# Cross-attention and FFN on one core: loops unrolled, tiles turned by transposing DMAs instead of TensorE, mask added by a matmul, projections woven into the softmax steps

## Chip, core and metric

The kernel runs on one core of a Trainium2 chip. The metric is the device time of one execution in microseconds (us). The kernel before takes 1211.33 us, the median of 3 runs (1210.6 to 1213.23).

## What is computed

For 16 sequences of 128 tokens with 1024 features (2048 rows in all) and a context of the same size:

```python
x = x + xattn(layernorm(x), ctx, ctx, w_q, w_k, w_v, w_out, mask)   # 32 heads of 32, 8 key/value groups of 4 heads
x = x + ffn(layernorm(x), w12, b12, w3, b3)
# xattn: softmax(where(mask, q k^T / sqrt(32), finfo.min)) v, then @ w_out.T
# ffn:   x1, x2 = split(x @ w12.T + b12); (silu(x1) * x2) @ w3.T + b3
```

Everything is float32. The kernel keeps that precision by splitting each operand of a matmul into a high and a low float16 part (hi = f16(v), lo = f16(v - hi)) and by summing three products, hi*hi + hi*lo + lo*hi. Weights and context are scaled by a power of two beforehand, which is found from their largest magnitude (the kernel calls that a "top").

## The kernel before, in words

**Attention** goes over 8 blocks of 256 tokens (two sequences). Block t is projected while block t-1 attends. One iteration of the loop has 12 steps; in step s TensorE computes the scores of head group s (`scores`, L855), turns the probabilities of group s-2 from [query, key] to [key, query] with 8 f32 transposes (`turn_prob`, L867), weighs the values of group s-3 (`weigh`, L883), turns the attention output of group s-4 (`turn_attn`, L894), and computes one unit of the projections of block t (`product`, L812, 24 matmuls: 8 chunks of the contraction by 3 products). After the 12 steps it turns the normalised rows of block t+1 (`turn_x`, 16 transposes, L910) and does the four units of the output projection of block t-1 in a row (`out_proj`, L812 on `arena_out`). Iterations 2 to 6 are one hardware loop (`Fori`), as on every engine.

VectorE adds the mask while it takes the row maximum, one instruction of 128x128 per head (`row_maxima`, L1145, 64 a block), ScalarE applies exp per head (`exps`, L661, 64 a block), and the high and low parts of the turned probabilities are made from PSUM (`prob_hi`, L670, ScalarE; `prob_lo`, L1157, VectorE). The q and k parts are stacked to 96 partitions (hi, lo, hi against hi, hi, lo) by 24 and 12 small DMAs per block (`stack_q`, L387; `stack_k`, L395), because the stacks put other partitions under each other. GpSimd splits the context with 3 instructions per quarter (`split_ctx`, L536 to L540) and takes the inverse square roots of the layernorm (L524).

**Weights.** wq, wk, wv and wo are split chunk by chunk between the projections of block 0 and in iteration 1 (`high` L614 on ScalarE, `chunk_lo` L1092 on VectorE); their largest magnitude goes through TensorE (`turn_top`, `spread_top`, L788, L792). For w12 one common scale is found by reading all of it once during iterations 2 to 6 (`look_at_w12`, L1251, a 128x4096 reduction each), and it is loaded again and split in iterations 7 and 8 and in the first FFN block.

**FFN** goes over 4 blocks of 512 rows: 16 units of `product` for the hidden layer (24 matmuls of 128x512 each), 16 transposes of the next block's rows (`turn_y`, L1009), one unit of the output, 16 more transposes, 7 more units of the output.

The order of the work on each engine is written out by hand. One DMA queue, SP's, issues all transfers in program order; a wait in it holds all that is behind. The PSUM banks are: two for scores, two for turned probabilities, one for `weigh`, one for turned attention, two for projections.

Of the kernel before, what the change touches and what calls it, by code (L numbers as in the profile page):

```python
# [17 lines left out]

# [11 lines left out]
RMAX = bass.bass_isa.ReduceOp.max  # L31
# [19 lines left out]
VW = DH + 2  # L51
# [12 lines left out]
NDMA_STACK = 12  # L64


def xattn_ffn(nc, x, ctx_t, mask, wq_t, wk_t, wv_t, wo_t, w12_t, b12_t, w3_t, b3_row, out):
    x_blocks = x.rearrange("(b u p) d -> b p u d", b=NB, p=P)
    x1_dram = nc.dram_tensor("x1_scratch", (TOK, D), F32, kind="Internal").ap()
    x1_blocks = x1_dram.rearrange("(b u p) d -> b p u d", b=NB, p=P)  # L70
    x1_ffn = x1_dram.rearrange("(b u p) d -> b p u d", b=NF, p=P)
    out_ffn = out.rearrange("(b u p) d -> b p u d", b=NF, p=P)

    def at(blocks, i):

        return blocks[bass.ds(i, 1)].rearrange("o p u d -> (o p) u d")

    with ExitStack() as stack:
# [5 lines left out]


        arena_in = sb("arena_in", [P, 32768], F16)
        arena_out = sb("arena_out", [P, 16384], F16)
        arena_work = sb("arena_work", [P, 32768], F16)
        wstage = sb("wstage", [P, 4096], F32)

        def carve(arena, at_, n, dt=F16):

            w = n * (2 if dt is F32 else 1)
            v = arena[:, at_:at_ + w]
            return (v.bitcast(dt) if dt is F32 else v), at_ + w

        o = 0
        wq, o = carve(arena_in, o, 2 * GROUPS * KC * P)
        wq = wq.rearrange("p (s m c o) -> p s m c o", s=2, m=GROUPS, c=KC)
        ctx_in, o = carve(arena_in, o, KC * AB, F32)  # L100
        wk, o = carve(arena_in, o, 2 * KC * KV)
        wk = wk.rearrange("p (s c o) -> p s c o", s=2, c=KC)
        wv, o = carve(arena_in, o, 2 * KC * KV)
        wv = wv.rearrange("p (s c o) -> p s c o", s=2, c=KC)
        ctx, o = carve(arena_in, o, 2 * KC * AB)
        ctx = ctx.rearrange("p (s c n) -> p s c n", s=2, c=KC)
        wo = arena_out[:, :].rearrange("p (h s c o) -> p h s c o", h=2, s=2, c=KC)
        w12 = arena_in[:, :].rearrange("p (m s c o) -> p m s c o", m=MC, s=2, c=KC)
        w3 = wo

        o = 0
        x_in, o = carve(arena_work, o, U * D, F32)
        x_in = x_in.rearrange("p (u d) -> p u d", u=U)
        x_res, o = carve(arena_work, o, U * D, F32)
        x_res = x_res.rearrange("p (u d) -> p u d", u=U)
        xn, o = carve(arena_work, o, 2 * KC * AB)
        xn = xn.rearrange("p (s c n) -> p s c n", s=2, c=KC)
        q_part, o = carve(arena_work, o, 2 * 2 * 4 * AB)  # L120
        q_part = q_part.rearrange("p (r s g n) -> p r s g n", r=2, s=2, g=4)
        assert o <= 2 * FT * D + 2 * KC * FB, o
        o = 2 * FT * D + 2 * KC * FB
        q_stack, o = carve(arena_work, o, HEADS * AB)
        q_stack = q_stack.rearrange("p (g j n) -> p g j n", g=GROUPS, j=HPG)
        k_stack, o = carve(arena_work, o, GROUPS * AB)
        k_stack = k_stack.rearrange("p (b g n) -> p b g n", b=2, g=GROUPS // 2)
        v_aug, o = carve(arena_work, o, 2 * U * GROUPS * VW)
        v_aug = v_aug.rearrange("p (s u g w) -> p s u g w", s=2, u=U, g=GROUPS)
        attn_t, o = carve(arena_work, o, 2 * GROUPS * AB)  # L130
        attn_t = attn_t.rearrange("p (s g n) -> p s g n", s=2, g=GROUPS)
        assert o <= arena_work.shape[1], o
        score = sb("score", [P, 4, U, HPG * SEQ], F32)
        prob_t = sb("prob_t", [P, 2, 2, U, HPG * SEQ], F16)
        attn = sb("attn", [P, 2, U * HPG * DH], F32)
        k_part = sb("k_part", [P, 2, 2, AB], F16)


        o = 0
        y_in, o = carve(arena_work, o, FT * D, F32)  # L140
        y_in = y_in.rearrange("p (u d) -> p u d", u=FT)
        yn, o = carve(arena_work, o, 2 * KC * FB)
        yn = yn.rearrange("p (s c n) -> p s c n", s=2, c=KC)
        hid, o = carve(arena_work, o, 2 * MC * FB)
        hid = hid.rearrange("p (s c n) -> p s c n", s=2, c=MC)
        y_res, o = carve(arena_work, o, FT * D, F32)
        y_res = y_res.rearrange("p (u d) -> p u d", u=FT)
        assert o <= arena_work.shape[1], o
        silu = prob_t[:, :, :, :, :].rearrange("p a b c d -> p (a b c d)")[:, 0:2 * 2 * FB].bitcast(F32) \
            .rearrange("p (r n) -> p r n", r=2)  # L150
        gated = score[:, 0, :, :]
        b3_all = score[:, 2, :, :].rearrange("p u n -> p (u n)")


        ident = sb("ident", [P, P], F32)
        mask_u8 = sb("mask_u8", [P, SEQ], U8)
        mask_add = sb("mask_add", [P, SEQ], F32)
        b12 = sb("b12", [P, 2 * MC], F32)
        b2_scaled = sb("b2_scaled", [P, MC], F32)
        NW = 5 + 2 + 4 + MC + 4  # L160
        NSCALE = NW - (MC - 1)
        CH_K, CH_V, CH_O = 3, 6, 7
        CH_12, CH_3 = CH_O + 4, CH_O + 4 + MC
        w_max = sb("w_max", [P, NSCALE], F32)
        w_top = sb("w_top", [P, NSCALE], F32)
        w_exp = sb("w_exp", [P, NSCALE], F32)
        w_inv = sb("w_inv", [P, NSCALE], F32)
        w_scale = sb("w_scale", [P, NSCALE], F32)
        ctx_max = sb("ctx_max", [P, 1], F32)
        ctx_top = sb("ctx_top", [P, 1], F32)  # L170
        ctx_exp = sb("ctx_exp", [P, 1], F32)
        ctx_inv = sb("ctx_inv", [P, 1], F32)
        ctx_scale = sb("ctx_scale", [P, 1], F32)
        score_base = sb("score_base", [P, GROUPS], F32)
        out_base = sb("out_base", [P, 4], F32)
        c_score = sb("c_score", [P, GROUPS], F32)
        c_neg = sb("c_neg", [P, GROUPS], F32)
        c_out = sb("c_out", [P, 4], F32)
        ctx_exp_kept = sb("ctx_exp_kept", [P, 1], F32)
        w12_part = sb("w12_part", [P, 1], F32)  # L180
        c_hid = sb("c_hid", [P, 1], F32)
        c_hid_inv = sb("c_hid_inv", [P, 1], F32)
        hid_scale = sb("hid_scale", [P, 1], F32)
        c_ffn = sb("c_ffn", [P, 4], F32)
        bound = sb("bound", [P, 8], F32)
        row_max = sb("row_max", [P, 4, U * HPG], F32)
        neg_max = sb("neg_max", [P, 4, U * HPG], F32)
        inv_sum = sb("inv_sum", [P, U * HPG], F32)
        stats = sb("stats", [P, 2, 6], F32)
        moments = sb("moments", [P, 2, 2], F32)  # L190
        var_scaled = sb("var_scaled", [P, 2], F32)
        rstd = sb("rstd", [P, 2], F32)
        minus_half = sb("minus_half", [P, 1], F32)
        ones = sb("ones", [1, P], F32)
        w_one = sb("w_one", [1, CH_12], F32)
        ctx_one = sb("ctx_one", [1, 1], F32)


        bank = [stack.enter_context(nc.psum_tensor(f"bank{i}", [P, HALF], F32)) for i in range(8)]
        B_SCORE, B_TURN, B_AV, B_ATTN_T, B_DENSE = bank[0:2], bank[2:4], bank[4], bank[5], bank[6:8]  # L200
        B_FFN = bank[4:8]
        B_XT = bank[0:4]


        s_mask, s_b12, s_b3 = sem("mask_loaded"), sem("b12_loaded"), sem("b3_loaded")
        s_wload = [sem(f"weights_loaded_{i}") for i in range(8)]
        s_wload += [sem(f"weights_loaded_{i}") if i in (11, 14, 15) else None for i in range(8, 16)]
        s_wlook, s_w12max, s_w12init = sem("w12_looked_at"), sem("w12_max_step"), sem("w12_max_init")
        s_wmax, s_wtop, s_wscale = sem("w_max_done"), sem("w_top_done"), sem("w_scale_done")
        s_wrow, s_wone, s_ctxrow, s_ctxone = sem("w_max_turned"), sem("w_one_done"), sem("ctx_turned"), sem("ctx_one_done")  # L210
        s_whi, s_wready = sem("w_hi_done"), sem("w_ready")
        s_wscaled, s_wpool = sem("w_scaled_on_pool"), sem("w_ready_on_pool")
        s_ident, s_vinit, s_ones = sem("ident_done"), sem("v_init_done"), sem("ones_done")
        s_xfirst = sem("first_row_tile_loaded")
        s_xload, s_ctxload, s_xres = sem("x_loaded"), sem("ctx_loaded"), sem("x_res_loaded")
        s_ctxmax, s_ctxtop, s_ctxscale = sem("ctx_max_done"), sem("ctx_top_done"), sem("ctx_scale_done")
        s_ctxhi, s_ctx = sem("ctx_hi_done"), sem("ctx_ready")
# [19 lines left out]

        block = stack.enter_context(nc.Block())

        def dense0(t):
# [1235 lines left out]
```

## Time and profile before

| | us |
|---|---|
| median of 3 runs | 1211.33 |
| the profiled execution, its own time | 1213.68 |
| its span, from the first to the last instruction | 1211.9 |
| TensorE busy in the span | 1136.6 (94%) |
| VectorE, ScalarE, GpSimd busy | 656.9, 457.2, 202.3 |
| mean granted TensorE clock, share of full speed | 0.965 |

A start-to-start time tells what a matmul costs in a stream of them; its own duration is longer, since matmuls overlap. The chain of waits merges them without overlap, so its pieces add up. Busy times of VectorE also count overlapping instructions once, so that single durations times their number can come to more than the busy time.

### The profile page before, as it was taken

The numbers are of one execution on the slowest core, as the hardware profiler recorded it, in microseconds if no ns is written. First come the engines' busy times: TensorE is split into PE (matmuls) and PEld (weight loads), VectorE is DVE, ScalarE is ACT, GpSimd is POOL, SyncE is SP. The second block draws the span as 40 slices with busy tenths as digits, with TensorE's granted clock in tenths as the row PEclk, the third lists the DMA queues.
The fourth block names the chain that finished last, engine by engine and source line by source line (L and its number), as shares of the span: only waits on it lengthen the run. The fifth ranks groups of instructions, "written<-read, shape, count | busy, mean of one in ns | idle before, by whom it ended". The sixth has DMA issues, their size and how long they took to land.

```text
span 1211.9 us, 22281 instructions
## 1 busy us (share of the span) xinstructions
PE 1136.6 (94%) x8377; PEld 719.4 (59%) x8377; DVE 656.9 (54%) x2130; ACT 457.2 (38%) x978; POOL 202.3 (17%) x167
## 2 busy tenths in 40 slices
PE   4768899999999999999986998899999999999998
PEld 3557759779596887958755443444445444544443
DVE  5468849688696877968798244631233123411111
ACT  3448719357291854818586112200111011101100
POOL 2304004031040402204143000400030003003000
PEclk9788899999999999999995998899999999999999
DMA  6442314323423333334360250004000300011001
GB/s 242 143 154 68 102 32 142 119 104 93 149 91 108 124 110 142 84 119 166 97 257 1 102 194 35 1 35 174 1 1 35 141 32 0 17 67 54 1 18 52
DMA packets 55113, 109.35 MB, mean 90 GB/s; under 512 B 6288, under 2 KB 37008, under 8 KB 50448
## 3 DMA queue, kind: packets, MB, share of 16 engines
q1 hardware_dynamic: 55056, 108.58, 25.8%
q8 instruction: 38, 0.62, 0.2%
q14 instruction: 19, 0.16, 0.0%
HBM read 76.05 MB, written 16.78 MB: 77 GB/s over the span
## 4 chain that ended last, share of the span: by engine, by line
PE 78%; DVE 11%; issue 5%; POOL 3%; ACT 3%; DMA 0%; DVEq 0%; ACTq 0%; POOLq 0%
PE bank L812 66%; PE bank L867 3%; DVE score L1145 2%; PE bank L883 2%; PE bank L910 2%; PE bank L855 1%; PE bank L894 1%; DVE stats L1098 1%; DVE prob_t L1157 1%; PE bank L1009 1%; ACT arena_in L614 1%; POOL arena_in L540 1%; DVE arena_out L1092 1%; POOL arena_in L536 1%; POOL arena_in L538 1%
## 5 line engine op out<-in xcount | busy, mean ns | idle before, releaser
L812 PE MATMUL bank<-arena_work,arena_in 128*128 128x256 f16 (+1 forms) x3072 | 529.4, 334 | 16.9 <-DVE arena_in L1092 8.7
L812 PEld LDWEIGHTS bank<-arena_work,arena_in 128*128 128x128 f16 x3072 | 306.1, 100 | 226.1 <-issue 20.4
L812 PE MATMUL bank<-arena_out,arena_work 128*128 128x512 f16 x1536 | 334.8, 379 | 0.1
L661 ACT ACTIVATE score<-score,neg_max,c_score 128x128 f32<-128x128 f32 x512 | 205.8, 497 | 148.7 <-DVE neg_max L1151 148.6
L812 PEld LDWEIGHTS bank<-arena_out,arena_work 128*128 128x128 f16 x1536 | 150.2, 98 | 178.0 <-issue 0.5
L1405 DVE SCALAR_TENSOR_TENSOR score<-bank,b_scaled,prob_t 128x512 f32<-128x512 f32 x32 | 24.0, 750 | 205.9 <-PE bank L812 197.3
L1145 DVE CUSTOM_DVE_ANT_0 score<-bank,mask_add 128x128 f32<-128x128 f32 x512 | 113.1, 287 | 18.0 <-PE bank L855 12.8
L524 POOL TENSOR_TENSOR rstd<-var_scaled,minus_half 128x1 f32<-128x1 f32 x32 | 29.4, 918 | 465.6 <-DVE var_scaled L1104 465.6
L759 ACT ACTIVATE prob_t<-bank,b,c_hid 128x512 f32<-128x512 f32 x32 | 24.8, 776 | 202.0 <-PE bank L812 202.0
L812 PE MATMUL bank<-arena_in 128*128 128x256 f16 x768 | 92.2, 278 | 2.6 <-issue 2.6
L1431 DVE SCALAR_TENSOR_TENSOR arena_work<-bank,c_ffn,arena_work 128x256 f32<-128x256 f32 x64 | 28.0, 479 | 118.3 <-PE bank L812 118.3
L1157 DVE TENSOR_TENSOR prob_t<-bank,prob_t 128x512 f16<-128x512 f32 x128 | 81.9, 680 | 9.3 <-ACT prob_t L670 9.1
L867 PE MATMUL bank<-ident,score 128*128 128x128 f32 x512 | 73.0, 286 | 12.5 <-DVE prob_t L1157 9.1
L812 PEld LDWEIGHTS bank<-arena_in 128*128 128x128 f16 x768 | 76.3, 100 | 12.8 <-issue 2.8
L762 ACT ACTIVATE arena_work<-score,hid_scale 128x512 f16<-128x512 f32 x32 | 23.1, 722 | 150.5 <-DVE score L1405 150.5
L536 POOL TENSOR_TENSOR arena_in<-arena_in,ctx_scale 128x512 f16<-128x512 f32 x32 | 34.3, 1070 | 258.7 <-DVE ctx_scale L1246 258.7
L670 ACT ACTIVATE prob_t<-bank 128x512 f16<-128x512 f32 x128 | 69.5, 596 | 10.7 <-PE bank L867 10.6
L867 PEld LDWEIGHTS bank<-ident,score 128*128 128x128 f32 x512 | 58.6, 146 | 16.1 <-ACT score L661 8.2
L1210 DVE SCALAR_TENSOR_TENSOR arena_work<-bank,c_out,arena_work 128x256 f32<-128x256 f32 x64 | 28.0, 479 | 72.4 <-PE bank L812 72.4
L883 PE MATMUL bank<-arena_work,prob_t 128*128 128x34 f16 x1536 | 49.5, 179 | 3.8 <-DVE arena_work L1210 2.4
L883 PEld LDWEIGHTS bank<-arena_work,prob_t 128*128 128x128 f16 x1536 | 48.9, 97 | 5.8 <-DVE arena_work L1210 2.6
L589 POOL TENSOR_TENSOR arena_work<-arena_work,score 128x1024 f32<-128x1024 f32 x16 | 39.4, 2495 | 62.7 <-DMA arena_work<-x_scratch 62.7
(104 smaller groups left out, 936.0 us busy)
## 6 DMA issues: line engine op xcount, KB each, us to landing
arena_work<-x SPq DMA_DIRECT2D x15, 1024.0 KB, 5.3
arena_work<-x_scratch SPq DMA_DIRECT2D x7, 2048.0 KB, 12.1
arena_work<-arena_work SPq DMA_DIRECT2D x192, 64.0 KB, 2.0
wstage<-w_t SPq DMA_DIRECT2D x5, 2048.0 KB, 7.6
wstage<-w_t SPq DMA_DIRECT2D x9, 1024.0 KB, 6.9
arena_in<-ctx_t SPq DMA_DIRECT2D x8, 1024.0 KB, 5.0
x_scratch<-arena_work SPq DMA_DIRECT2D x8, 1024.0 KB, 4.0
out<-arena_work SPq DMA_DIRECT2D x16, 512.0 KB, 2.6
```

The lines of the kernel that those rows point to most:

```text
L524: pool.tensor_tensor(rstd[:, r:r + 1], var_scaled[:, r:r + 1], minus_half[:, :], ALU.pow)\
L536: pool.tensor_tensor(hi, ctx_in[:, cols], spread, ALU.mult).then_inc(s_ctxhi, 1)
L589: ins = pool.tensor_tensor(y_res[:, u], y_res[:, u], b3_all, ALU.add)
L661: ins = act.activation(s, s, ACT.Exp, bias=neg_max[:, m % 4, HPG * u + j:HPG * u + j + 1], scale=c_score[:, m:m + 1])
L670: act.activation(prob_t[:, m % 2, 0, u], B_TURN[u][:, :], ACT.Copy).then_inc(s_pthi, 1)
L812: ins = pe.matmul(dst, lhs(a, c), rhs(b, c), start=(c == 0 and n == 0), stop=(c == KC - 1 and n == 2))
L867: ins = pe.transpose(B_TURN[u][:, SEQ * j:SEQ * j + SEQ], score[:, m % 4, u, SEQ * j:SEQ * j + SEQ], ident[:, :])
L883: ins = pe.matmul(dst, prob_t[:, m % 2, p, u, SEQ * j:SEQ * j + SEQ], v_aug[:, v, u, m], start=(n == 0), stop=(n == 2))
L1145: ins = dve.tensor_tensor_reduce(score[:, m % 4, u, SEQ * j:SEQ * j + SEQ], B_SCORE[u][:, SEQ * j:SEQ * j + SEQ], mask_add[:, :], 1.0, MAS ...
L1157: dve.tensor_tensor(prob_t[:, m % 2, 1, u], B_TURN[u][:, :], prob_t[:, m % 2, 0, u], ALU.subtract)\
L1210: ins = dve.scalar_tensor_tensor(out=cols, in0=B_DENSE[q % 2][:, 256 * n:256 * n + 256], scalar=c_out[:, 2 * h + n:2 * h + n + 1], in1=col ...
L1431: ins = dve.scalar_tensor_tensor(out=cols, in0=B_FFN[q % 4][:, 256 * k:256 * k + 256], scalar=c_ffn[:, 2 * h + k:2 * h + k + 1], in1=cols, ...
```

## The change

It rewrites the program. No engine has a loop any more. A block has 8 steps, and a hand-made list (`dense_order`) gives the order of all projection units, tops and FFN units, which take turns in three PSUM banks; a unit waits until the unit three before it has been read. In step s, TensorE does the scores of group g, then two dense units, then `weigh(g - 2)`. `out_proj` of block b runs in steps 3 to 6 of iteration b+2, one unit each, no longer four in a row. The first hidden units of the FFN run in iteration 8 (`H_AT`).

- The transposes `turn_prob`, `turn_attn`, `turn_x`, `turn_y` on TensorE are gone. The f32 tile is split into high and low f16 parts first, side by side, and a DMA on SP's queue (`dma_start_transpose`) writes them turned: 128x2048 f16 (512 KB) per group for the probabilities, 128x512 (128 KB) per group for the attention output, 128x2048 (512 KB) per tile of 128 rows.
- The mask is a bf16 matmul of the identity with the mask repeated four times (128x512) into each score bank, ahead of the four score matmuls. The row maximum is one reduction of 128x1024 a group, and exp reads PSUM.
- q and k parts are written to DRAM and read back into the stacks: for each half of q one store and 3 loads, the same for k (16 DMAs a block in place of 36).
- Every chunk of w12 and w3 gets a scale of its own, found by a look at it (12 looks of 1 MB in iterations 2 to 5). ctx, wo 0 and 1, w12 0 to 5 and w3 are split in place by GpSimd (multiply, copy, subtract per 512 columns). w12 6 and 7 are split after the attention.
- v's low part has no column of ones any more (33 and 32 columns instead of 34).

The core of the diff:

```diff
-                turn_x(t + 1, attend)
-                if not (isinstance(t, int) and t == NB - 1):
-                    for q in range(4):
-                        out_proj(t, q, 12 + q if project else q)
...
+            def turn_prob(g):
+                sp.wait_ge(s_plo, g + 1)
+                if g >= 2:
+                    sp.wait_ge(s_av, g - 1)
+                sp.dma_start_transpose(prob_t[:, g % 2].rearrange("p u s j n -> p (u s j) n"),
+                                       p_split[:, g % 2].rearrange("p u s n -> p (u s n)"))\
+                    .then_inc(s_pturn[g % 2], 16)
...
+            for t in range(1, NB + 1):
+                a = t - 1
+                for s in range(STEPS):
+                    g, now = GROUPS * a + s, STEPS * t + s
+                    if g >= 1:
+                        turn_prob(g - 1)
+                    if g >= 3:
+                        turn_attn(g - 3)
+                    if s == 0:
+                        stack_k(a, 1)
+                        stack_q(a, 1)
+                    if t < NB and s == 0:
+                        load_ctx(t)
+                    if t < NB - 1 and s in (1, 2):
+                        load_tile(2 * t + 1 + s)
...
+                    if t < NB and s in (2, 5):
+                        spill_q(t, int(s == 5))
+                    if t < NB and s == 4:
+                        stack_q(t, 0)
+                    if t < NB and s in (6, 7):
+                        spill_k(t, s - 6)
+                    if t < NB and s == 7:
+                        stack_k(t, 0)
...
+                    if t < NB - 1 and s in (5, 6):
+                        turn_tile(2 * t + s - 3)
...
+                for u in range(U):
+                    pe.matmul(B_SCORE[g % 2][:, HALF * u:HALF * u + HALF].rearrange("p (j n) -> p j n", j=HPG),
+                              ident_bf[:, :], mask_bf[:, :].rearrange("p (o n) -> p o n", o=1)
+                              .broadcast_to([P, HPG, SEQ]), start=True, stop=False)
...
+            def weigh(g):
+                a, m = g // GROUPS, g % GROUPS
+                pe.wait_ge(s_pturn[g % 2], 16 * (g // 2 + 1))
...
+                dve.tensor_reduce(row_max[:, g % 2, :], B_SCORE[g % 2][:, :].rearrange("p (h n) -> p h n", n=SEQ), AX_X,
+                                  ALU.max).then_inc(s_rmax, 1)
...
+                pool.tensor_tensor(buf, src, spread, ALU.mult).then_inc(s_pool, 1)
+                pool.wait_ge(s_pool, chain[0] + 1)
+                pool.tensor_copy(hi, buf).then_inc(s_pool, 1)
+                pool.wait_ge(s_pool, chain[0] + 2)
+                pool.tensor_tensor(lo, buf, hi, ALU.subtract).then_inc(ready, 1)
```

## Rows read from the trace of the kernel before

**Rows 1.** The page, part 1: busy time of each engine, share, instructions.
```profile
PE 1136.6 (94%) x8377; PEld 719.4 (59%) x8377; DVE 656.9 (54%) x2130; ACT 457.2 (38%) x978; POOL 202.3 (17%) x167
```
**Rows 2.** The page, part 4: the chain that ended last, shares by engine.
```profile
PE 78%; DVE 11%; issue 5%; POOL 3%; ACT 3%; DMA 0%; DVEq 0%; ACTq 0%; POOLq 0%
```
**Rows 3.** Busy time by stretch: length, PE, PEld, DVE, ACT, POOL, granted clock, DMA share, GB/s.
```profile
0.00:84.20 84.20, 54.24 (x348) 42.33 (x349) 44.31 (x90) 34.44 (x45) 19.82 (x27) 0.88 0.50 172
84.20:178.70 94.50, 81.69 (x754) 61.64 (x752) 67.67 (x251) 56.48 (x117) 18.38 (x14) 0.93 0.26 79
...
251.00:323.30 72.30, 72.07 (x743) 56.99 (x740) 56.43 (x222) 40.62 (x104) 14.43 (x14) 1.00 0.35 114
...
540.20:686.30 146.10, 126.79 (x1188) 93.50 (x1186) 114.39 (x440) 94.41 (x204) 39.85 (x24) 0.87 0.32 115
686.30:784.60 98.30, 90.14 (x401) 40.44 (x400) 44.67 (x61) 20.70 (x22) 13.39 (x12) 0.93 0.27 102
...
912.40:1040.30 127.90, 127.90 (x612) 59.95 (x610) 34.96 (x60) 16.10 (x26) 13.39 (x8) 1.00 0.13 49
```
**Rows 4.** The chain of waits by time (start, us, what), one block of the loop.
```profile
230.28 20.73 PE bank L812 x96
...
281.02 0.45 PE bank L855 x8
281.47 0.88 PE bank L867 x8
282.35 0.59 PE bank L883 x24
282.94 0.27 PE bank L894 x2
283.21 2.62 PE bank L812 x24
...
300.85 1.75 PE bank L910 x16
```
**Rows 5.** Groups by shape in the block 302.6 to 374.9: busy us, mean ns, idle before.
```profile
L661 ACT ACTIVATE score<-score,neg_max,c_score 128x128 f32<-128x128 f32 x64 | 25.7, 503 | 23.7 <-DVE neg_max L1151 23.7
...
L1145 DVE CUSTOM_DVE_ANT_0 score<-bank,mask_add 128x128 f32<-128x128 f32 x64 | 14.1, 286 | 1.5 <-PE bank L855 1.2 <-DVE ctx_exp_kept L1223 0.3
...
L1157 DVE TENSOR_TENSOR prob_t<-bank,prob_t 128x512 f16<-128x512 f32 x16 | 10.2, 680 | 1.6 <-ACT prob_t L670 1.6
...
L1251 DVE TENSOR_REDUCE w_part<-wstage 128x1 f32<-128x4096 f32 x1 | 4.4, 4409 | 0.0
...
L1228 DVE TENSOR_REDUCE ctx_max<-arena_in 128x1 f32<-128x2048 f32 x1 | 2.3, 2276 | 0.0
```
**Rows 6.** Groups by shape on ScalarE and GpSimd, whole span.
```profile
L614 ACT ACTIVATE arena_in<-wstage,w_scale 128x1024 f16<-128x1024 f32 x6 | 6.8, 1142 | 2.5 <-DVE w_scale L1087 2.5
...
L620 ACT ACT_TABLE_LOAD x1 | 1.3, 1283 | 0.7 <-PEq L1472 0.7
...
L536 POOL TENSOR_TENSOR arena_in<-arena_in,ctx_scale 128x512 f16<-128x512 f32 x32 | 34.3, 1070 | 258.7 <-DVE ctx_scale L1246 258.7
```
**Rows 7.** SP's queue by time: start, us of issuing, what, how many.
```profile
324.46 0.41 SPq L409 DMA_DIRECT2D x_scratch<-arena_work  x1
...
344.56 7.72 SPq L387 DMA_DIRECT2D arena_work<-arena_work  x12
```
**Rows 8.** The page, part 6: DMA issues, KB each, median us to landing.
```profile
arena_work<-x SPq DMA_DIRECT2D x15, 1024.0 KB, 5.3
...
arena_work<-arena_work SPq DMA_DIRECT2D x192, 64.0 KB, 2.0
...
out<-arena_work SPq DMA_DIRECT2D x16, 512.0 KB, 2.6
```
**Rows 9.** Busy time by stretch, while the 12 stack DMAs run, and while a 2 MB load runs (columns as in rows 3).
```profile
344.60:352.30 7.70, 7.70 (x113) 7.20 (x112) 7.59 (x43) 7.70 (x21) 1.99 (x2) 1.00 0.36 85
...
305.80:314.00 8.20, 8.20 (x40) 3.72 (x38) 4.07 (x6) 0.00 (x0) 0.00 (x0) 1.00 0.69 260
```

More of the change, by code:

```diff
@@ new lines, with done, look_at, max_order @@
+DENSE = {key: i for i, key in enumerate(dense_order())}
+def done(*key):
+    return DENSE[key] + 1
+LOOK_AT = {3: "w{0}", 5: "w3{2}", 7: "w{1}"}
+def look_at(t, s):
+    return LOOK_AT[s].format(2 * (t - 2), 2 * (t - 2) + 1, t - 2) if 2 <= t < 6 and s in LOOK_AT else None
+def max_order():
+    n = ["ctx0"]
+    for t in range(1, NB):
+        for s in range(STEPS):
+            if s == 1:
+                n.append(f"ctx{t}")
+            if look_at(t, s):
+                n.append(look_at(t, s))
+            if t == NB - 1 and s == 3:
+                n.append("b12")
+    return n
@@ L187, in xattn_ffn @@
[L187 to L199, printed above, removed]
@@ L542, in iteration @@
-            def iteration(t, tops=(), los=(), los_after=()):
-                if not (isinstance(t, int) and t == NB):
-                    for k in range(4):
-                        split_ctx(t, k)
-                for n in tops:
-                    top(n)
-                for n in los:
-                    chunk_lo(n)
-                for u in range(U):
-                    root(2 * t + 2 + u, u)
-                for n in los_after:
-                    chunk_lo(n)
+            chain, free = [0], {}
@@ L801, in spread_ctx_top, with begin @@
-            def spread_ctx_top(t):
-                pe.wait_ge(s_ctxone, t + 1)
-                dst = top_bank("ctx") if isinstance(t, int) and t == 0 else B_AV
-                pe.matmul(dst[:, 0:1], ones[:, :], ctx_one[:, :], start=True, stop=True).then_inc(s_ctxtop, 1)
+            order = [0]
+            def begin(*key):
+                n = DENSE[key]
+                assert n == order[0], (key, n, order[0])
+                order[0] += 1
+                if n >= 3:
+                    pe.wait_ge(s_dread, n - 2)
+                return bank(*key)
@@ new lines, in turn_top, with spread_top @@
+            def turn_top(name, count, signal):
+                at, k = COL[name]
+                pe.wait_ge(signal, count)
+                dst = begin("turn", name)
+                pe.transpose(dst[0:k, 0:P], w_max[:, at:at + k], ident[:, :]).then_inc(s_dense, 1)
+            def spread_top(name):
+                k = COL[name][1]
+                pe.wait_ge(s_diag, spread_count(name))
+                dst = begin("spread", name)
+                pe.matmul(dst[:, 0:2 * k], ones[0:k, :], diag[0:k, :, 0:k], start=True, stop=True).then_inc(s_dense, 1)
```

2122 lines of the change are left out of this document (1061 added, 1061 removed), and 3 rows, old and new, of the table n.

## The prediction

> **What bounds the kernel now.** I read the busy times first: TensorE is busy 1136.6 of 1211.9 us [rows 1], so whatever ends at it counts, and the others have room. The chain of waits agrees: 78% of it is TensorE, 11% VectorE, 5% issue [rows 2]. The stretches say where the rest is [rows 3]. A middle block takes 72.3 us with TensorE busy 72.07 at full clock: there only removed TensorE work shortens anything. At the start (84.2 us, TensorE busy 54.24 at clock 0.88), in iteration 1 (94.5), in iterations 7 and 8 (146.1, busy 126.79, clock 0.87) and in the first hidden layer (98.3) it waits for the splits of weights and for a softmax chain with nothing beside it. A middle FFN block is 127.9 us of TensorE and nothing else.
>
> **TensorE's pieces** [rows 4]: scores of a group 0.45, turned probabilities 0.88, weighing 0.59, turned attention output 0.27, a q unit of 24 matmuls 2.62, 96 matmuls of 512 columns 20.73 (0.216 each, 5.18 a unit), turned rows 1.75 per 16.
>
> **A middle block after.** Out go 8 x 0.88 + 8 x 0.27 + 1.75 = 10.9 us of transposes. In come 16 mask matmuls of 512 columns, 16 x 0.216 = 3.5, and about 0.9 for three more tops (each a transpose and a small matmul, an estimate from the 0.27 of two transposes). 72.3 - 10.9 + 3.5 + 0.9 = 65.8 us, if TensorE stays the bound. Its cover elsewhere:
>
> VectorE had 56.43 of 72.3. Its 64 masked maxima are busy 14.1 us; a reduction costs 2.28 us for 2048 columns and 4.41 for 4096 [rows 5], so 1.2 for 1024, 8 x 1.2 = 9.7. The low parts of the probabilities stay at 10 (10.2 for 16 of 512). The looks grow from 4.4 to 3 x 2.28 = 6.8, tops add about 3.5. Net 56.4 - 14 + 9.7 + 2.4 + 3.5 = 58 of 65.8: it hides, with little room in the steps that hold a look, and I add 1.5 us to each of blocks 2 to 5 for that. ScalarE had 40.62; exp is unchanged (25.7 a block), the high parts become 8 pieces of 1024 at 1.14 [rows 6], 9 us, in place of 16 of half the width: hidden. GpSimd adds a copy per 512 columns at some 1.07 [rows 6]; its ctx work was 14.43 of 72.3: hidden.
>
> **The transposing DMA** is the term that decides, and no row shows one. Call p the time that SP's queue needs for one of 512 KB, issue or transfer, whichever is longer. From below: a store issues in 0.41 us [rows 7] and 512 KB land in 2.6 [rows 8], so p is 2 to 2.6 at best. By bytes: the stack DMAs bring 64 KB in 7.72/12 = 0.64 us each [rows 7], 512 KB would be p = 5.1. From above: 2048 columns are 16 squares of 128, and if each is issued as such a DMA, p = 16 x 0.64 = 10.3. I take p = 3: it is nearest to the 512 KB transfer, being as wide and as contiguous on the source side. A block needs 8 p for probabilities, 2 p for the attention output (a quarter of the bytes each) and 2 p for two row tiles, and 26 plain DMAs, 12 stack loads at 0.65 and 14 others at 0.41, 13.5 us: 12 p + 13.5, so 49.5 at p = 3, under 65.8. The wait of `weigh(g - 2)` has two steps (13 us) from the low parts to its use: hidden at p = 3. What is late next is the first scores of a block: SP issues turn, turn, `spill_k`, `stack_k` in step 7 (which is short, 0.9 + 2 x 2.62 + 0.6 = 6.7 us), and the stack must land (2.0 us, [rows 8]) before the next block. I count 2 us for each of 8 boundaries, 16 in all. As to the data engines: they are 0.36 busy at 85 GB/s under stack DMAs, 0.69 at 260 under a load [rows 9], so full at 236 to 377; a block moves some 16 MB in 67 us, 240 GB/s. There is no room to spare at the lower rate.
>
> The Trainium skill speaks for it in "Advanced Engine Details and Errata", section X-Bar Transpose (TRN2): transposing DMAs are said to be as fast as regular ones; by that p would be 2.6 and the sum 3 us lower. No row here shows it.
>
> **Sum, in us of span.** Start to the first scores 73: SP holds ctx and half of wq behind the first two row turns (about 12 + 2 x 3 + 1 = 19 us), after which 3 MB, then k and v, arrive at the start's 172 to 220 GB/s, v by 50; splits, v unit and k stack take 20 more. That is 84.2 plus 3 us before. Iteration 1: its own TensorE work is 44.6, but VectorE has some 54 with two wo chunks: 57. Iterations 2 to 5: 4 x (65.8 + 1.5) = 269. Iterations 6 and 7: 132. Boundaries: 16. Iteration 8: three short steps of 6.7 with a hidden unit, two of 11.9, four that carry `out_proj`, with 0.9 + 0.6 + 5.2 each, 64, plus 2 for six table loads of 1.28 [rows 6], as silu stands between exps in steps 0, 2 and 7: 66. The splits of w12 on GpSimd (12 x 1.07 = 13 us a chunk) start two steps before and stay ahead of one chunk per 14 us. Then 6 hidden units, 4 of out, 4 of hidden at 5.2: 74. First output 41.5. Three FFN blocks of 127.9 - 3.5 = 124.4: 373. For the last row tile of each, which is split at the seventh output unit and turned by about its end: 3. After the last matmul 4, as now. 73 + 57 + 269 + 132 + 16 + 66 + 74 + 41.5 + 373 + 3 + 4 = 1108.5. The profiled execution took 1213.68, 1.8 above its span and 2.35 above the median of 1211.33; so 0.5 comes off for a median: 1108.
>
> **The rivals.**
>
> *Queue-bound, still faster.* At p = 5.1 SP needs 12 x 5.1 + 13.5 = 75 us a block, 6 more than 67.3 + 2, in 7 blocks 40, in iteration 1 18, at the start 8 and in the FFN 6: 1108 + 72 = 1180. For it: the many small pieces of a turned tile look more like the stack's. Against: rows of 4 KB on the source. 0.20.
>
> *Slower.* One mechanism: SP's queue in `turn_prob`. All its terms are about 100 p - 436 above the sum for large p, which reaches the 103 us of the gain at p = 5.4. From there each group of TensorE work waits in `weigh`. At p = 7 it is 1108 + 264 = 1372; at 10.3 some 1700. For it: nothing in this trace turns through a DMA, TensorE does it at 0.11 us a square [rows 4], and SP is one queue that holds all that is behind. Against: the upper bound assumes one issue per square. 0.26.
>
> Here a page speaks against the change. The Trainium skill, "VectorE: DVE Perf Modes", section The three transpose paths, gives 1309 ns for a 128x128 square by DMA against 390 on TensorE. If squares did not overlap, 16 would be 21 us, far beyond 5.4; if that is one DMA's fixed latency, it changes nothing. No row tells.
>
> *TensorE-bound but for weaker reasons shorter or longer:* VectorE's fixed order makes blocks 70 instead of 67.3 (+15), or clock drops at the boundaries; both stay inside the forecast's own range. That the transposes are gone but their time returns in full as waits is 0.02, within 0.2%.
>
> **How the numbers follow.** Forecast (TensorE-bound, p up to about 4) 0.52, own range 1080 to 1145; queue-bound 0.20, up to 1209; slower 0.26; same 0.02. Faster by over 0.2% is 0.52 + 0.20 = 0.72. A measurement of this kernel can tell about 0.2% from no change, 2.4 us; its three runs spread 2.6. The range goes from 1085 (boundaries and start free) to 1225: it takes in all of the second case and the edge of the slower one, and leaves out 0.03 below and about 0.2 above.
>
> **What would show it.** Right: middle blocks of 66 to 69 us with TensorE over 95% busy at clock 1.00, FFN blocks of 124 to 126, the transposing DMAs' issue under 4 us. Wrong: TensorE idle before `weigh` with the DMA of `prob_t` as releaser, SP's queue issuing without a break, a granted clock below 1 in the middle. Wrong in the start: the first scores after 85 us. The forecast falls if p is above 4.5.

## The result, and the profile after the change

The changed kernel takes 1249.6 us in the median of four runs (1246.08 to 1252.88), beside 1212.07 for the kernel before on the same chip: a ratio of 1.031, with a 95% interval of 1.0276 to 1.0343. The forecast was 1108, the range ended at 1225. The change makes the kernel 3% slower, and the prediction was wrong in sign.

The page after the change, busy times, granted clock, DMA engines and queues:

```profile
span 1245.6 us, 18812 instructions
PE 1077.6 (87%) x7633; PEld 636.0 (51%) x7633; DVE 607.4 (49%) x1106; ACT 437.6 (35%) x882; POOL 315.6 (25%) x293
PEclk9896898889889889798887999999999999999999
DMA  9576688887969879679869767426300620061001
DMA packets 277925, 181.08 MB, mean 145 GB/s; under 512 B 239056, under 2 KB 249296, under 8 KB 272976
q1 hardware_dynamic: 277840, 179.89, 58.1%
```

TensorE's work did shrink, from 1136.6 us [rows 1] to 1077.6, although its clock was lower in the loop. VectorE has room. So the time is in neither engine's work. What grew is in the lines on DMA: five times as many packets as before (55,113 then), 86% of them under 512 bytes, and the DMA engines at six to nine tenths through the whole loop. Their share is the time that packets take, added up and divided by sixteen times the stretch.

Busy time by stretch after the change (columns as in [rows 3]); the stretches are the start, iterations 1 to 8, the rest of the first FFN block in two pieces, and a stretch as long as an FFN block. TensorE's stream shows that the first FFN block ends at 868.5, so the last two lines are cut 3.5 us late:

```profile
0.00:73.30 73.30, 44.69 (x307) 34.06 (x308) 43.37 (x93) 42.08 (x55) 18.69 (x25) 0.91 0.77 248
73.30:145.10 71.80, 45.70 (x519) 38.57 (x520) 53.72 (x83) 42.67 (x94) 39.89 (x35) 0.84 0.69 151
145.10:233.60 88.50, 72.60 (x665) 51.27 (x666) 56.37 (x105) 40.62 (x94) 17.57 (x18) 0.90 0.82 188
233.60:323.40 89.80, 73.23 (x669) 51.76 (x669) 57.28 (x111) 40.63 (x94) 14.75 (x14) 0.90 0.81 190
323.40:412.90 89.50, 72.30 (x668) 51.35 (x669) 57.28 (x111) 40.36 (x94) 14.75 (x14) 0.90 0.84 190
412.90:500.60 87.70, 71.97 (x669) 51.18 (x670) 57.19 (x111) 40.64 (x94) 14.76 (x14) 0.91 0.84 194
500.60:583.50 82.90, 70.00 (x662) 50.40 (x663) 53.44 (x102) 41.35 (x95) 15.06 (x15) 0.91 0.77 174
583.50:682.60 99.10, 71.86 (x662) 51.08 (x663) 53.02 (x110) 40.73 (x95) 32.69 (x36) 0.84 0.84 198
682.60:745.00 62.40, 59.46 (x457) 30.89 (x458) 38.60 (x58) 38.32 (x80) 56.03 (x52) 0.95 0.75 154
745.00:850.00 105.00, 105.00 (x551) 48.58 (x550) 39.64 (x62) 23.63 (x31) 52.59 (x51) 1.00 0.48 146
850.00:872.00 22.00, 21.23 (x99) 9.53 (x98) 9.39 (x19) 2.11 (x2) 1.46 (x2) 1.00 0.67 176
872.00:996.60 124.60, 124.60 (x579) 56.47 (x578) 33.95 (x56) 16.23 (x20) 13.82 (x8) 1.00 0.24 70
```

Against the terms of the sum, each of which had its boundary and row-tile wait in it:

| stretch | forecast, us | measured, us | difference |
|---|---|---|---|
| start to the first scores | 73 | 73.3 | +0.3 |
| iteration 1 | 57 + 2 | 71.8 | +12.8 |
| iterations 2 to 5 | 269 + 8 | 355.5 | +78.5 |
| iterations 6 and 7 | 132 + 4 | 182.0 | +46.0 |
| iteration 8, hidden and first output | 66 + 2 + 74 + 41.5 | 185.9 | +2.4 |
| three FFN blocks and the end | 373 + 3 + 4 | 377.1 | -2.9 |

The differences add up to 137 us, the whole error of the span (1245.6 for 1108.5). It lies in the attention loop. A middle block takes 89.5 us, where TensorE had 65.8 to do: in the block 412.90:500.60, of 87.7 us, TensorE idles before three instructions, and is busy 72 in place of 66 because its granted clock is 0.91. The three, in the timeline (start, length, instruction, idle time before it and who ended it):

```profile
412.92 0.59 PE L960 MATMUL bank_score<-arena_in 128*128 128x512 bf16 x1 [7.94 <-issue]
435.06 0.37 PE L907 MATMUL bank_dense<-arena_in 128*1 128x128 f32 x1 [5.68 <-DVE arena_in L1143]
459.71 0.38 PE L913 MATMUL bank_dense<-small,arena_in 1*128 1x2 f32 x2 [2.94 <-DVE small L1131]
```

These are the block's first scores, the turn of the context's maximum, and the spread of a weight's maximum. None of them is `weigh` waiting for turned probabilities. The first line is the wait ahead of this block, the other two lie in it. The first two trace back to SP's queue (start, length of the issue, DMA):

```profile
399.58 0.39 SPq L429 DMA_DIRECT2D k_scratch<-arena_in  x1
400.06 5.25 SPq L401 DMA_TRANSPOSE arena_rows<-arena_rows  x1
405.40 2.01 SPq L443 DMA_TRANSPOSE arena_attn<-arena_attn  x1
407.50 1.64 SPq L451 DMA_TRANSPOSE arena_attn<-arena_in  x1
409.23 0.53 SPq L429 DMA_DIRECT2D k_scratch<-arena_in  x1
409.86 1.38 SPq L436 DMA_DIRECT2D arena_attn<-k_scratch  x3
...
418.38 1.78 SPq L443 DMA_TRANSPOSE arena_attn<-arena_attn  x1
420.26 1.79 SPq L451 DMA_TRANSPOSE arena_attn<-arena_in  x1
422.14 1.49 SPq L436 DMA_DIRECT2D arena_attn<-k_scratch  x3
423.73 1.38 SPq L421 DMA_DIRECT2D arena_attn<-q_scratch  x3
425.15 0.43 SPq L407 DMA_DIRECT2D arena_in<-ctx_t  x1
425.68 6.78 SPq L443 DMA_TRANSPOSE arena_attn<-arena_attn  x1
```

The keys' first half was stored at 399.58. Its three loads into the stack are issued at 409.86, behind a turned row tile that takes 5.25 us to issue and two more turns, and the last lands at 412.8; TensorE had finished the block at 405.

Why those issues are so long can be read beside the landings. The row tile's issue ends at 405.31; the look at a weight that was issued ahead of it lands at 404.99 and the store of the keys at 405.45. The next turn's issue ends at 407.41, and the row tile lands at 407.38. The issue of 6.78 us ends at 432.46, and the context lands at 432.69. It is so throughout: of the 64 DMAs that turn 512 KB of probabilities, 22 were issued while an earlier transfer still had over 2.5 us to go. Their issues took 2.9 to 9.0 us and ended within 0.6 us of its landing. The turns of 128 KB in the same queue took 1.2 to 2.0 us, whatever was under way. So here a turn of 512 KB holds SP's queue until what is ahead of it has landed.

The context is asked for at 425.15, last in its step, though its buffer was free at about 404, and VectorE then waits for it. In iteration 1 a wait of another kind stands: 16.14 us before the keys' projection, ended by GpSimd (L605), whose split of the context stood in its queue behind the root for row tile 5.

The transposing DMAs themselves, all 64 of the probabilities (the source view, issue in ns min/median/max, then issue to landing in us):

```profile
L443 SPq DMA_TRANSPOSE arena_attn<-arena_attn x64: 1317/1987/8952, 84.1 to 756.0; - x64
DMA to landing us min/median/max: 4.3/4.6/11.1
```

So a turn's issue was 1.3 to 2.0 us where nothing was under way ahead of it, and up to 9 where something was; the mean is 2.9.

### The profile page after: what moved, and what is told of

It is laid out like the page before. It is cut to its first block and busy times, and to the rows that moved or that the text cites. A ratio compares the mean times of both kernels' runs of the same rounds, so it can differ in the third digit from the quotient of the medians.

```text
span 1245.6 us, 18812 instructions
## 1 busy us (share of the span) xinstructions
PE 1077.6 (87%) x7633; PEld 636.0 (51%) x7633; DVE 607.4 (49%) x1106; ACT 437.6 (35%) x882; POOL 315.6 (25%) x293
## 5 line engine op out<-in xcount | busy, mean ns | idle before, releaser
L920 PE MATMUL bank_dense<-arena_rows,arena_in 128*128 128x256 f16 (+1 forms) x2304 | 371.5, 324 | 3.3 <-DVE arena_in L1148 3.3
L920 PEld LDWEIGHTS bank_dense<-arena_rows,arena_in 128*128 128x128 f16 x2304 | 236.0, 104 | 123.8 <-DVE arena_in L1148 3.7
L750 ACT ACTIVATE arena_attn<-bank_score,arena_in 128x128 f32<-128x128 f32 x512 | 191.2, 468 | 90.5 <-DVE arena_in L1224 90.4
L920 PE MATMUL bank_dense<-arena_out,arena_attn 128*128 128x512 f16 x768 | 179.6, 393 | 2.9 <-issue 2.9
L920 PE MATMUL bank_dense<-arena_out,arena_in 128*128 128x512 f16 x768 | 166.1, 379 | 0.8 <-issue 0.8
L920 PE MATMUL bank_dense<-arena_attn,arena_rows 128*128 128x512 f16 x768 | 166.4, 379 | 0.0
L920 PEld LDWEIGHTS bank_dense<-arena_out,arena_attn 128*128 128x128 f16 x768 | 76.5, 101 | 94.2 <-issue 14.9
L920 PE MATMUL bank_dense<-arena_in 128*128 128x256 f16 x768 | 91.1, 279 | 18.6 <-POOL arena_in L605 16.1
L1221 DVE TENSOR_REDUCE arena_in<-bank_score 128x8 f32<-128x1024 f32 x64 | 78.1, 1220 | 45.8 <-PE bank_score L964 44.5
L1229 DVE TENSOR_TENSOR arena_attn<-arena_attn 128x1024 f16<-128x1024 f32 x64 | 77.7, 1214 | 1.5 <-ACT arena_attn L759 1.5
L605 POOL TENSOR_TENSOR arena_in<-arena_in 128x512 f16<-128x512 f32 x56 | 76.2, 1360 | 4.5
```

The lines of the kernel that those rows point to most:

```text
L605: pool.tensor_tensor(lo, buf, hi, ALU.subtract).then_inc(ready, 1)
L750: ins = act.activation(e[:, g % 2, u, SEQ * j:SEQ * j + SEQ], B_SCORE[g % 2][:, SEQ * h:SEQ * h + SEQ], ACT.Exp, bias=neg_max[:, g % 2, h: ...
L920: ins = pe.matmul(dst, lhs(a, c), rhs(b, c), start=(c == 0 and n == 0), stop=(c == KC - 1 and n == 2))
L1221: dve.tensor_reduce(row_max[:, g % 2, :], B_SCORE[g % 2][:, :].rearrange("p (h n) -> p h n", n=SEQ), AX_X, ALU.max).then_inc(s_rmax, 1)
L1229: dve.tensor_tensor(p_split[:, g % 2, :, 1], e[:, g % 2], p_split[:, g % 2, :, 0], ALU.subtract)\
```

## The experiments

Two theories. **A, order:** the DMAs on which TensorE waits stand too late in SP's queue (and GpSimd's split too late in its own). **B, load:** the DMA engines themselves have more work than the block gives them time for, and the order only decides who is seen waiting. The forecast had 2 us at each block's boundary for A and nothing for B.

Kernel before in the same session: 1213.15 us beside e1 to e4, 1210.97 beside e5 to e8, 1212.74 beside e9 to e11. All ratios are to it. The times are medians of 8 executions for e1, e2 and e3, of 4 for e4 and e11, and of only 2 for e5 to e10.

### e1_ctx_first: the context's load first in its step

```diff
+                    if t < NB and s == 0:
+                        load_ctx(t)
                     if g >= 1:
                         turn_prob(g - 1)
...
                         stack_q(a, 1)
-                    if t < NB and s == 0:
-                        load_ctx(t)
```

> Only the place of one DMA in SP's queue changes: the context of block t is issued first in step 0, ahead of the turned probabilities and the stacks, not behind them. Theory A (the order in SP's queue makes the waits, the DMA engines could do it): the wait of TensorE for the context's maximum, 5.0 to 7.1 us in each of 7 blocks, falls below 1 us, and some clock comes back: about 1205 to 1215 us. Rival B (the DMA engines are full, 0.81 to 0.84 busy in a middle block, so order only moves waits): the wait at the block's start grows by what this one loses, 1240 to 1250 us.

Measured: 1218.94 us (1214.56 to 1223.64), ratio 1.0048 (1.0028 to 1.0068). Moving one DMA ahead of eight others takes 2.5% off the changed kernel. TensorE's wait at the context's maximum falls to 2 us or less in iterations 2 to 5 (up to 3.3 later), not below 1; the block's first scores still wait 7.1 to 7.8, and the spread 4.1. The time is 4 us over theory A's range and far under B's. The middle block 313.65:397.38 is 83.7 us.

### e2_feed_first: also the row tile and the stack of keys first

```diff
+                    if t < NB and s == 7:
+                        stack_k(t, 0)
+                    if t < NB - 1 and s in (5, 6):
+                        turn_tile(2 * t + s - 3)
                     if g >= 1:
                         turn_prob(g - 1)
```

with the same lines taken out further down, on top of e1.

> As e1, and what the next block waits for goes first in its step too: the turned row tiles first in steps 5 and 6, the k stack first in step 7. Theory A: the wait of 7.1 to 7.9 us before each block's first scores falls to under 3 us as well, middle blocks from 89 to about 73 us, 1250 - 7 x 15 = about 1145 us. Rival B: blocks stay above 83 us, 1210 us or more.

Measured: 1202.36 us (1196.76 to 1206.27), ratio 0.9902 (0.9881 to 0.9922). Three moves in one queue turn the change from 3.1% slower into 1% faster. The first scores now wait 1.7 to 3.9 us. But the wait at the context's maximum is back at 2.2 to 4.7 us. The time lies between the two expectations, the middle block is still 16.6 us longer than TensorE's 65.8, and the DMA share has risen:

```profile
303.31:385.75 82.44, 70.16 (x668) 49.98 (x669) 57.02 (x111) 39.47 (x94) 14.77 (x14) 0.96 0.93 206
```

### e3_half_turned: half of the turned bytes, order as changed

```diff
-                sp.dma_start_transpose(prob_t[:, g % 2].rearrange("p u s j n -> p (u s j) n"),
-                                       p_split[:, g % 2].rearrange("p u s n -> p (u s n)"))\
+                sp.dma_start_transpose(prob_t[:, g % 2, 0].rearrange("p s j n -> p (s j) n"),
+                                       p_split[:, g % 2, 0].rearrange("p s n -> p (s n)"))\
```

The second sequence is weighed with the first one's probabilities.

> The order of the queue is that of the changed kernel, but only the first sequence's probabilities of a group are turned (256 KB in place of 512 KB), and the second sequence is weighed with the first's; all matmuls stay. It leaves out half of the turned probabilities. Theory A (order): the wait for the context stays about 5 us, since nothing ahead of its issue waits for the data engines, and the wait at a block's start falls from 7.2 by 1 to 2 us; 1225 to 1240 us. Rival B (bytes through the DMA engines): both waits shrink in step with the load, DMA share from 0.83 to about 0.65, 1180 us or less.

Measured: 1216.63 us (1209.82 to 1221.26), ratio 1.0027 (1.0002 to 1.0052). It is under theory A's range and far above B's. The order is the same; the waits before the first scores (4 to 6 us) are shorter, those at the context (3.5 to 6.9) hardly. So 256 KB a group less is worth about as much as e1's move. But the edit takes away more than bytes. A turn of 256 KB is issued in 1.24 us in the median, 3.3 at most, also with transfers under way, so it does not hold the queue; SP issues for 46 us in place of 61 in the middle block. That belongs to A as much as to B.

### e4_quarter_look: plain bytes less, order as changed

```diff
-                sp.dma_start(look, weights).then_inc(s_look, 16)
+                sp.dma_start(look[:, 0:512], weights[:, 0:512]).then_inc(s_look, 16)
```

The maxima are taken over what lies in the buffer, of which a quarter is newly loaded.

> The 12 looks at w12 and w3 load 256 KB in place of 1 MB; the reduction over them stays as long. It leaves out three quarters of what the scales are found from. Theory A: 0 to 15 us less (the look stands right ahead of a turned row tile in step 6). Rival B: 9 MB less through engines that are full, 9 MB at some 200 GB/s is 45 us less, in blocks 2 to 5 alone.

Measured: 1224.05 us (1220.3 to 1228.51), ratio 1.0084 (1.0036 to 1.0132). The wait at the spread of a weight's maximum is mostly gone, those at the context (4.7 to 7.7 us) and the first scores (4.6 to 7.5) remain. The 25.5 us less lie between A's 0 to 15 and B's 45. After these four neither theory can stand alone: on the same kernel, order gives 4% and either kind of bytes 2 to 3%.

### e5_pool_mixed: GpSimd's order, and six loads spread out

```diff
                     root(2 * t + 2)
+                    split_ctx(t, range(3))
                     root(2 * t + 3)
+                    split_ctx(t, range(3, 4))
                 if t == NB - 1:
                     root(2 * NB + 1)
-                split_ctx(t)
+                    split_ctx(t)
...
+W12_LOAD = [STEPS * (NB - 1) + i for i in (5, 6, 8, 9, 11, 12)]
```

on top of e2; iteration 7 keeps its split whole.

> This is e2_feed_first with two further edits. GpSimd does three quarters of the split of a block's context before the second row tile's root of the variance (before, the split stood behind both roots), and the six weight loads of 1 MB at the end of iteration 7 and the start of iteration 8 are spread over six steps, where they were two to a step. Theory A, the order of the queues: GpSimd's split in iteration 1 starts at the context's scale, near 95 us, and not at 103, so TensorE's wait of 15.6 us ahead of the keys' projection falls to 5 to 8; its wait at the start of iteration 8 (8.6 us) falls to 3 or less; the time falls by 12 to 18 us from 1202.4, to 1184 to 1190. Theory B, the load on the DMA engines is what the loop now runs at: iteration 1's wait falls, but the time comes back as waits for transfers in the next two iterations, and the time stays at 1195 or more.

Measured: 1191.20 us (1189.67 to 1192.73), ratio 0.9837 (0.9778 to 0.9896), between the two expectations. In iteration 1 the 15.6 us wait becomes 2.4 before the keys and 4.0 before a `weigh`, and the iteration falls from 66.1 us (in e2) to 62.8; iteration 7 falls from 94.1 to 89.4; the wait at the start of iteration 8 is 5.6 in place of 8.6. Blocks 2 to 5 are as they were (328 us in all, 330 in e2).

### e6_tops_late: the small matmuls later in TensorE's order

```diff
-                units = turn + units[:1] + spread + units[1:]
+                units = units[:1] + turn + units[1:] + spread
```

with TensorE's and VectorE's programs to match, and GpSimd's root of row tile 2 NB + 2 ahead of the last split.

> As e5_pool_mixed, with the two small matmuls of each maximum moved on in TensorE's order: the turn goes behind the step's first projection, the spread behind its last, and VectorE's steps for them move with them. Theory A: the waits of TensorE at the context's turn (3.7 us a block) and at the spread (4.1 us in the blocks that look at a weight) go, some 5 to 7 us for each of five blocks; the middle block, 82.4 us, comes to 75 to 78 and the time to 1155 to 1165. Theory B (the DMA engines carry the block at its length): the middle block stays within 1.5 us of 82.4, and the same time is seen as a wait for turned probabilities, a turned row tile or the stack of keys; the time stays within 8 us of e5_pool_mixed's.

Measured: 1183.63 us (1182.74 to 1184.52), ratio 0.9775 (0.9721 to 0.9828). The wait at the context's turn is gone from all blocks, and the first scores' wait has grown from 2.4 to 3.1 us to 4.8 to 6.5. The wait at the spread did not go: 3.4 to 4.4 us in blocks 2 to 5. This is what theory B said: 7.6 us in all, 81.0 us for each of blocks 2 to 5 after 82.1. The wait moved on.

### e7_spill_first: the keys' first half stored earlier

```diff
+                    if t < NB and s == 6:
+                        spill_k(t, 0)
                     if t < NB - 1 and s in (5, 6):
                         turn_tile(2 * t + s - 3)
...
-                    if t < NB and s in (6, 7):
-                        spill_k(t, s - 6)
+                    if t < NB and s == 7:
+                        spill_k(t, 1)
```

> As e6_tops_late, with the store of the keys' first half put first in SP's step 6, ahead of the turned row tile (7.2 us of issue at most) and the turned probabilities. Theory A: the stack of keys is issued some 3 us earlier, and the wait of 2.7 to 3.9 us at the start of each block falls to under 1; the time falls by 12 to 20 us from e6_tops_late's. Theory B: the store waits in the DMA engines in place of SP's queue and lands little earlier, under 5 us in all.

Measured: 1169.16 us (1167.2 to 1171.13), ratio 0.9655 (0.9592 to 0.9718), 14.5 less than e6, as theory A had it in size; but the wait it was to remove is still 4.5 to 5.7 us in the middle. Blocks 2 to 5 are 2.4 us shorter each with the earlier store. Half of that is TensorE's busy time, 70.1 for 71.3 on average at a clock of 0.94 for 0.92, and half shorter waits. The packets now take 0.97 of the block, 76 of 78.4 us:

```profile
291.90:370.32 78.42, 70.45 (x669) 51.10 (x670) 57.74 (x112) 39.64 (x94) 13.59 (x14) 0.94 0.97 217
370.32:448.24 77.92, 70.66 (x668) 51.11 (x669) 59.20 (x113) 39.80 (x94) 13.60 (x14) 0.94 0.97 218
```

### e8_spill_half_turned: e7 with half of the turned bytes

The edit of e3, on e7; the second sequence is again weighed with the first one's probabilities.

> As e7_spill_first, and only the first sequence's probabilities are turned (256 KB in place of 512 KB for each group): the second sequence is weighed with the first's, so half of the attention's output is not the reference's. Theory A (order alone was left): the time stays within 5 us of e7_spill_first's. Theory B (the load on the DMA engines): half of these bytes gone gives 3 us or more in each of seven blocks, 20 to 40 us, and the granted clock of the middle blocks comes to 0.99 or more, with TensorE's gaps under 3 us a block.

Measured: 1122.34 us (1119.46 to 1125.21), ratio 0.9268 (0.9195 to 0.9342), 47 us below e7: more than what the same edit gave with the old order (33), and more than B's 20 to 40. The middle block is 71.2 us at clock 0.98, its first scores wait 2.2 to 3.0. As in e3, the turns no longer hold the queue (1.24 us of issue in the median, 2.97 in e7), and SP issues for 48 us of the block in place of 63:

```profile
275.39:346.86 71.47, 67.98 (x668) 49.61 (x669) 57.04 (x112) 39.80 (x94) 13.66 (x14) 0.98 0.88 209
```

### e9_plain_copy: the same bytes, not turned

```diff
-                sp.dma_start_transpose(prob_t[:, g % 2].rearrange("p u s j n -> p (u s j) n"),
+                sp.dma_start(prob_t[:, g % 2].rearrange("p u s j n -> p (u s j n)"),
```

on e7: the attention is weighed with unturned probabilities.

> As e7_spill_first, but the DMA of a group's probabilities copies them as they lie (512 KB, 4 KB in each partition) and does not turn them, so the attention is weighed with unturned probabilities and its output is not the reference's. Theory B1 (the engines are taken by the small packets, 2048 of 256 bytes for each of these DMAs, some 3 us of all engines): the copy is cheaper, the DMA share of a middle block falls from 0.97 to 0.85 or less, the block comes to 69 to 73 us, and the time falls by 25 to 50 us from 1169. Theory B2 (the bytes count, turned or not; the transposing form is as fast as a plain one): the middle block stays at 76 to 78 us and the time within 8 us of 1169.

Measured: 1116.34 us (1115.11 to 1117.57), ratio 0.9205 (0.9186 to 0.9224), 51 us below the kernel with turning in the same session (e11, 1167.67). The page of e9, packets and queue, and its landing time, under them those of e7:

```profile
DMA packets 154021, 181.08 MB, mean 163 GB/s; under 512 B 106960, under 2 KB 117200, under 8 KB 149072
q1 hardware_dynamic: 153936, 179.89, 57.4%
arena_attn<-arena_attn SPq DMA_DIRECT2D x64, 512.0 KB, 3.5
```

```profile
DMA packets 277925, 181.08 MB, mean 155 GB/s; under 512 B 239056, under 2 KB 249296, under 8 KB 272976
q1 hardware_dynamic: 277840, 179.89, 62.4%
arena_attn<-arena_attn SPq DMA_TRANSPOSE x64, 5.5
```

The bytes are the same; 123,904 packets are gone, 1936 for each of 64 DMAs. The queue's packets took 0.624 x 1164.8 = 727 us of all engines in e7 and 0.574 x 1112.7 = 639 here: 1.4 us less a DMA. The trace's packets agree: in the block of the changed kernel 323.40:412.90, 256-byte packets take 24 ns each, so the 2048 of one turn make 3.1 us on sixteen engines; the 4 KB packets take 201 ns here, so the 128 of one copy make 1.6. It also lands 2.0 us sooner. Block and time fell as B1 said, the DMA share less: to 0.88 here, with 0.97 and 0.94 in the blocks beside it. B2 is out. But a copy's issue is 0.5 us where a turn's is 3.0, and SP issues for 45 us of the block in place of 63; how much of the 51 us is packets and how much a queue that isn't held was not separated. With 2.9 us of waits left, TensorE's work is seen nearly bare, at clock 1.00:

```profile
273.14:342.49 69.35, 66.42 (x668) 48.78 (x669) 57.24 (x112) 39.97 (x94) 13.67 (x14) 1.00 0.88 244
```

### e10_best_quarter_look: plain bytes less, on e7

The edit of e4; the maxima are again taken over what lies in the buffer.

> As e7_spill_first, and each of the twelve loads for a weight's maximum brings 256 KB in place of 1 MB, so a block of iterations 2 to 5 moves 2.25 MB less, some 6 to 8 us of its DMA engines; the maxima are taken over what lies in the buffer, so scales can differ from the reference's. If the load on the DMA engines sets the block, whoever makes the load: blocks 2 to 5 come from 78 to 72 to 74 us, the DMA share falls to about 0.93, and the time by 18 to 28 us to 1141 to 1151. If the transposing DMAs alone are what the loop waits for: under 8 us.

Measured: 1152.85 us (1152.04 to 1153.66), ratio 0.9506 (0.9488 to 0.9524), 14.8 below e11. That is less than the 18 to 28 expected, and far more than the under 8 of the other theory; iterations 2 to 5 fall from 314.6 us (in e7) to 299.0, so all of it is where the loads were. So plain bytes lengthen the loop too, not the turned ones alone. In e7 the stack of keys is issued right behind such a load, at 364.19, and its last part lands only at 370.23, 0.7 us after the load; the first scores wait for it. That a look placed behind the stack would have done as much was not tried.

```profile
282.98:355.71 72.73, 66.49 (x669) 48.81 (x669) 57.96 (x113) 40.70 (x98) 14.63 (x14) 1.00 1.00 201
```

The share is 1.00, not 0.93 as expected, with 14.6 MB moved in 72.7 us: the 256-byte packets took 27 ns each in place of 25 in e7. So the share doesn't fall in step with the bytes.

### e11_best_again: e7 in more rounds

> The kernel of e7_spill_first again, in more rounds, to have its interval: 1165 to 1173 us, a ratio of 0.962 to 0.970 to the kernel before.

Measured: 1167.67 us (1165.22 to 1169.62), ratio 0.9627 (0.9609 to 0.9645). With the changed kernel's operations as they are, and only the order in which the engines and queues take them mended, it beats both: 3.7% below the kernel before and about 6.5% below the changed one (0.9627/1.031 = 0.934).

## Why the prediction was wrong

**The step that failed** is the one that begins "The transposing DMA is the term that decides". It priced the DMAs as time of SP's queue alone, 12 p + 13.5, and took the DMA engines up only as a remark: "full at 236 to 377; a block moves some 16 MB in 67 us, 240 GB/s. There is no room to spare at the lower rate". The remark was right and got no term in the sum. A block moved 17 MB at a share of 0.84, so its packets took 0.84 x 89.5 = 75 us of all engines, above TensorE's 65.8. Before they took 0.35 x 72.3 = 25 [rows 3]. Half of the 75 is turning: 8 DMAs of probabilities, 8 quarters and 2 row tiles are twelve times 2048 packets of 256 bytes, 37 us together; the other 38 are loads, looks, stores and stacks. As a rate that is 190/0.84 = 226 GB/s, just under the lower end; this is an estimate, since it takes the share to grow in step with the bytes, which e10 speaks against. e7, with the waits ordered away as far as was tried, stays at 78 us with packets for 76; e8, e9 and e10 shorten it from three sides, whichever bytes or packets go.

**How the miss divides.** The median missed the forecast by 142 us. Order alone took back 80 of them (1249.6 to 1169.2, e1 to e7). Copying in place of turning took 51 more (e9 against e11), and some 8 to 10 are left. The first part is shown to be order. The second is load or the holding of SP's queue by turns of 512 KB: e3, e8 and e9 took away both, and e10, which took away plain bytes alone, also let the looks land sooner.

**p = 3** was near as a mean: 2.9 us of issue, 3.1 of the engines' packets. But it isn't one number: 1.3 to 2.0 with nothing ahead, up to 9 when held. And the queue's sum was short: SP issued for 61 us in the block 323.40:412.90, 46 of them for turns, where 12 p + 13.5 gave 49.5. It still had 28 us to spare, so the queue-bound rival and the slower one did not come about as written. Nearly nothing waits in `weigh`: the source view puts 3.1 us of TensorE's idle time in the whole run down to the probabilities' DMA. The kernel is slower by another road, and the 0.26 on slower was right only in its direction. The 3 us that p = 2.6 was to take off the sum come from no term of it: there p stands in the start alone, as 2 x 3.

**The boundary, 2 us** was mis-sized: 7.1 to 7.9 ahead of iterations 2 to 7 and 12.3 ahead of the last. The step had named the right DMA and the right queue, and left out the turned row tile in front, whose issue of 5.25 us waits for the look ahead of it to land. e2, which moves both ahead, brings the wait to 1.7 to 3.9.

**"What is late next"** was answered too narrowly, with the stack alone. The context's load, moved behind a step's turns, made TensorE wait 5.0 to 7.1 us a block (e1), and the spread of a weight's maximum 2.9 to 3.8, with VectorE waiting in order for a look's load (e4). The 1.5 us added for VectorE's order covers neither.

**Iteration 1, 57 us:** VectorE's 53.7 came as summed, but GpSimd's queue had no term, and its 16.14 us are the miss (e5).

**The clock, 1.00 in the middle:** TensorE was granted 0.90 in these blocks. Its busy time of 72 us against 66.4 in e9, for the same instructions, is 6 us a block that no wait shows. The levels are 1.2 and 2.4 GHz. In the block 412.90:500.60 the clock is at the lower one until 415.9, from 432.9 to 439.8, from 460.3 to 463.7 and from 497.8 on, each time from within a wait or just behind it: 16 us in all, and full between them.

**What was right:** TensorE's work of a block, 65.8, is 66.4 in e9 and 66.5 in e10 at clock 1.00. The start (73.3 for 73), an FFN block (124.3 for 124.4), VectorE's 58 us of a block (57.3). The row tile waits of the FFN (3 us) did not show.

On the two pages: the Trainium skill, "Advanced Engine Details and Errata", section X-Bar Transpose (TRN2), has transposing DMAs as fast as regular ones. e7 and e9 do not agree, 5.5 us to land for 3.5, and some 3.1 us of the engines for 1.6. The 1309 ns for a square of 128 in "VectorE: DVE Perf Modes", section The three transpose paths, is no price per square here: sixteen squares in one DMA land in 4.6 us.

**Still open:** whether the last 51 us are the engines' load or the held queue. The kernel that would tell turns the same bytes in two DMAs of 256 KB, which held nothing in e3 and e8; it was not run. Nor was a kernel tried that gives part of the turning back to TensorE, which has 12 us a block to spare in e7; each 512 KB so given back would free some 3.1 us of the DMA engines, by the packets above.

## What to carry to other kernels

When a change moves work to DMAs, write a line for the DMA engines like that for any other engine: bytes at the rate that this trace shows for that packet size, summed over a block, against the block's length. If the sum is near or over it, expect waits that the order in the queue moves and shortens. Put the transfer on which the next block's first instruction waits ahead of the bulk ones, and look at what stands before it, not only at when it is ready. Read each long issue beside the landing of what was issued ahead of it: that tells whether a DMA holds the queue. A wait that vanishes and comes back elsewhere (e6) is a reason to look at the load, but no proof that order is used up: the next move of order (e7) gave 14.5 us.

## What the runs showed of the hardware that was not expected

A transposing DMA of 512 KB of 16-bit words between two SBUF regions moves in 2048 packets of 256 bytes, and takes about twice the engine time of a plain copy of the same bytes with 4 KB in each partition (some 3.1 and 1.6 us of all sixteen). Its issue on SP takes 1.3 to 2.0 us with nothing ahead; with transfers under way it ends about when the last of them lands, up to 9 us later. Turns of 256 KB (e3, e8) and 128 KB did not wait so: 1.2 us in the median and 1.2 to 2.0 us. Most plain DMAs' issues stayed at 0.4 to 0.6, the longest at 1.9. And short waits cost TensorE twice: in the changed kernel, with some 16 us of waits a block, the granted clock is 0.90; in the block of e10 above, with 6 us in waits of 3.3 at most, it is 1.00.
